# Opening of a fused attention and mixture-of-experts kernel: first tokens loaded first and in halves, two of four norms on VectorE, two Toeplitz matrices loaded directly, the transposes of the queries ahead of the first unit

## The reference

```python
q  = layernorm(x)                       # over the 256 positions
kv = einsum('bhil,bhjl->bijhl', ctx, ctx)        # 16 heads of 8 channels
y  = causal_convolution(kv, ssm_kernel) + kv * D # along l, one filter and one D per head
x  = x + tanh(g_xattn) * einsum('bijhl,bihl->bjhl', y, q)
x  = x + tanh(g_ffn) * (experts(layernorm(x)) + shared_expert(layernorm(x)))
```

## Time and profile before

| what | value |
|---|---|
| median of 3 runs | 236.66 us (236.22 to 240.86) |
| profiled execution | 237.96 us, its span 236.1 us |
| PE busy | 199.6 us (85%) |
| DVE busy | 146.7 us (62%) |
| POOL busy | 121.3 us (51%) |
| ACT busy | 81.8 us (35%) |
| DMA | 31.87 MB, 135 GB/s over the span |

### The profile page before, as it was taken

One profiled execution on the slowest core, in us unless ns is written; L12 is line 12 of the kernel. 1 busy time (PEld: TensorE's weight loads), 2 busy tenths in 40 slices (PEclk: granted clock), 3 DMA queues, 4 the chain that ended last, 5 costly groups with the idle time before them and its releaser, 6 DMA issues.

```text
span 236.1 us, 3938 instructions
## 1 busy us (share of the span) xinstructions
PE 199.6 (85%) x1344; PEld 180.4 (76%) x1344; DVE 146.7 (62%) x479; ACT 81.8 (35%) x155; POOL 121.3 (51%) x125
## 2 busy tenths in 40 slices
PE   0195699977999799999999899897879989999940
PEld 0173579966999699898998898795779989899830
DVE  2508689589788987579855844652455665556220
ACT  2071440517434471333333165131443234423100
POOL 1497755267754789415850270260353757545642
PEclk9999799999999999999999999999999999999995
DMA  6599972000000020020501994897524798431311
GB/s 209 144 326 370 390 269 89 0 0 0 4 3 3 0 90 3 0 90 3 178 0 64 326 270 170 264 306 220 159 66 107 230 292 241 165 109 59 94 38 44
DMA packets 23925, 31.87 MB, mean 135 GB/s; under 512 B 3214, under 2 KB 21398, under 8 KB 23904
## 3 DMA queue, kind: packets, MB, share of 16 engines
q1 hardware_dynamic: 21312, 24.77, 33.2%
q0 software_dynamic: 2304, 6.05, 7.6%
q10 hardware_dynamic: 288, 0.79, 1.0%
HBM read 21.32 MB, written 10.54 MB: 135 GB/s over the span
## 4 chain that ended last, share of the span: by engine, by line
PE 63%; DMA 13%; issue 7%; DVE 7%; ACT 3%; SPq 2%; POOL 2%; POOLq 1%; DVEq 0%; ACTq 0%
PE fb L1084 12%; PE z L1000 10%; PE tp L1023 9%; PE z L1084 8%; PE z L1098 7%; PE fb L1098 7%; PE z L997 6%; DMA x_sb<-x 4%; DMA kv<-xd_scratch 4%; DMA xd_scratch<-xrow,dest 2%; DVE terms L428 2%; PE tp L1109 1%; DMA kskip_scratch<-kp 1%; ACT wh_gu L730 1%; DVE stats L782 1%
## 5 line engine op out<-in xcount | busy, mean ns | idle before, releaser
L428 DVE TENSOR_TENSOR terms<-z,qr 128x512 f32<-128x512 f32 (+2 forms) x192 | 48.8, 327 | 15.3 <-PE z L1000 8.5
L997 PE MATMUL z<-kv,toep 128*128 128x144 f32 x128 | 28.4, 305 | 19.4 <-DMA toep<-kskip_scratch 11.1
L997 PEld LDWEIGHTS z<-kv,toep 128*128 128x128 f32 x128 | 23.3, 200 | 26.9 <-issue 20.5
L1000 PE MATMUL z<-kv,toep 128*128 128x288 f32 x128 | 43.6, 424 | 0.0
L409 POOL TENSOR_TENSOR kv<-ct 128x768 f32<-128x768 f32 x15 | 28.1, 1871 | 16.4 <-PE z L1000 14.9
L1084 PE MATMUL fb<-xTh,wh_gu 128*128 128x256 f32 (+1 forms) x104 | 32.4, 311 | 1.8 <-issue 1.8
L1084 PE MATMUL fb<-xTl,wh_gu 128*128 128x256 f32 (+1 forms) x104 | 29.0, 279 | 0.0
L1084 PE MATMUL fb<-xTh,wl_gu 128*128 128x256 f32 (+1 forms) x104 | 29.0, 279 | 0.0
L619 POOL DMA_INDIRECT kv<-base_scratch,tok x16 | 19.8, 1235 | 16.0 <-DMA base_scratch<-x_sb 10.6
L630 POOL DMA_INDIRECT out<-kv,tok x16 | 16.1, 1004 | 21.9 <-DVE kv L887 18.7
L1084 PE MATMUL z<-xTh,wh_gu 128*128 128x256 f32 (+1 forms) x88 | 26.0, 295 | 1.2 <-DVE xTl L904 1.2
(11 more groups left out here) (108 smaller groups left out, 382.8 us busy)
## 6 DMA issues: line engine op xcount, KB each, us to landing
terms<-w SPq DMA_DIRECT2D x16, 352.0 KB, 4.6
...
```

The source lines that it names most:

```text
L428: return eng.tensor_tensor(view(terms, t0 + row * TROW + col, [[64, 2], *td]), view(src, zo, [[512, 2], *zd]), view(qr, q0 + qo, [[CW, 2], ...
L997: pe.matmul(view(z[s % 2], k * 512 + GB, [[PL, NPL], [1, GB]]), toep[:, h, P:2 * P], view(kv, o, [[PL, NPL], [1, GB]]), start=True, stop=F ...
L1000: mm = pe.matmul(z[s % 2][:, k, 0:KVH], toep[:, h, 0:P], view(kv, o, [[1, KVH]]), start=False, stop=True, skip_group_check=True)
```

## The change

Seven edits, all of them ahead of slot 4:

1. x of group 0 is SP's first transfer and comes as two transfers of two sequences (`x_half`, `x_in[0]`). DVE takes the statistics of the first two when the first is there. Filters and D are issued by ACT, ahead of the context.
2. The Toeplitz matrices of heads 0 and 1 are loaded straight from the filters as they come in, and D is put on their diagonals in SBUF: DVE adds `anti` (a matrix with ones where the diagonal lies, made by POOL) times D to the left half of each. The load through HBM covers heads 2 and 3, then four heads each as before.
3. x of group 1 is issued before the store of the corrected filters. The context of group 1 is issued ahead of the matrices of heads 8 to 15, and the three small loads behind them.
4. ACT norms two of the first four sequences, DVE the other two (`tensor_scalar`, a new line), after DVE's planes.
5. POOL makes `anti`, and computes one power of ones ahead of the first real one.
6. PE turns the queries of group 0 ahead of the convolution of slot 0.
7. ACT's tanh of the gates stands in slot 4 in place of ahead of slot 0.

The store of the filters has 768 KB more ahead of it on this queue than before, and the context and x of group 1 have moved up. The diff, without the declarations and the renumbered waits on POOL's constants:

```diff
@@ -383,6 +390,8 @@
 
             what, g = norms[n]
             eng.wait_ge(xn_done if what == "ln1" else xrow_done, g + 1)
+            if n == 0:
+                eng.wait_ge(xn_dve, 1)
 
         def load_rows(sp, e):
             if e == 0:
@@ -453,13 +462,18 @@
                 sp.dma_start(ct[:, g % 2, :], ctxt[g]).then_inc(ctx_in[g], 16)
 
             def load_x(g):
+                if g == 0:
+                    for i, done in ((0, x_half), (2, x_in[0])):
+                        sp.dma_start(x_sb[:, i:i + 2, :], x[i:i + 2].rearrange("b c l -> c b l")).then_inc(done, 16)
+                    return
                 sp.dma_start(x_sb[:, GB * g:GB * (g + 1), :],
                              x[GB * g:GB * (g + 1)].rearrange("b c l -> c b l")).then_inc(x_in[g], 16)
 
             def load_toeplitz(k):
 
-                src = bass.AP(kskip.tensor, kskip.offset + 4 * k * KPAD, [[1, P], [KPAD, 4], [1, L]])
-                sp.dma_start(toep[:, 4 * k:4 * k + 4, :], src).then_inc(toep_in[k], 16)
+                h, n = (4 * k, 4) if k else (2, 2)
+                src = bass.AP(kskip.tensor, kskip.offset + h * KPAD, [[1, P], [KPAD, n], [1, L]])
+                sp.dma_start(toep[:, h:h + n, :], src).then_inc(toep_in[k], 16)
 
             def load_gu(dst, a1, a3, done):
                 for m, a in ((0, a1), (1, a3)):
@@ -487,20 +501,22 @@
                 load_gu(gu_set[e % SETS], w1[e], w3[e], gu_in[e % SETS])
                 load_tail(down_set[e % SETS], w2[e], down_in[e % SETS], 0)
 
-            sp.dma_start(kp[:, :], kpad).then_inc(skip_in, 16)
-            sp.dma_start(dcol[:, :], bass.AP(skip_d.tensor, skip_d.offset, [[1, H], [1, 1]])).then_inc(skip_in, 16)
             load_x(0)
+            sp.dma_start(d_bc[:, :], bass.AP(skip_d.tensor, skip_d.offset, [[0, P], [1, 2]])).then_inc(d_in, 16)
+            sp.dma_start(toep[:, 0:2, :],
+                         bass.AP(kpad.tensor, kpad.offset, [[1, P], [KPAD, 2], [1, L]])).then_inc(toep_first, 16)
+            load_x(1)
             sp.wait_ge(skip_added, 1)
             sp.dma_start(kskip, kp[:, :]).then_inc(skip_stored, 16)
             sp.wait_ge(skip_stored, 16)
             load_toeplitz(0)
+            load_toeplitz(1)
+            load_ctx(1)
+            load_toeplitz(2)
+            load_toeplitz(3)
             sp.dma_start(gates[:, 0:1], bass.AP(g_x.tensor, g_x.offset, [[0, P], [1, 1]])).then_inc(small_in, 16)
             sp.dma_start(gates[:, 1:2], bass.AP(g_f.tensor, g_f.offset, [[0, P], [1, 1]])).then_inc(small_in, 16)
             sp.dma_start(wg_sb[:, :, :], wg.rearrange("(k p) e -> p k e", p=P)).then_inc(small_in, 16)
-            for k in range(1, 4):
-                load_toeplitz(k)
-            load_ctx(1)
-            load_x(1)
             load_shared_gu()
             load_tail(shared_down, sw2, shared_down_in, AGAIN)
             load_x(2)
@@ -552,6 +568,11 @@
             chain(pool.memset(ident[:, :], 0.0))
             pool.affine_select(out=ident[:, :], in_=ident[:, :], compare_op=ALU.not_equal, fill=1.0, base=0,
                                pattern=[[-1, P]], channel_multiplier=1).then_inc(pool_consts, 1)
+            chain(pool.memset(anti[:, :], 0.0))
+            pool.affine_select(out=anti[:, :], in_=anti[:, :], compare_op=ALU.not_equal, fill=1.0, base=1 - P,
+                               pattern=[[1, P]], channel_multiplier=1).then_inc(pool_consts, 1)
+            chain(pool.memset(rstd[:, :], 1.0))
+            chain(pool.tensor_tensor(rstd[:, :], rstd[:, :], rstd[:, :], ALU.pow))
             pool.wait_ge(dve_consts, 5)
             scale_and_bias(0)
             kv_place_free(pool, 0, 1)
@@ -638,7 +659,7 @@
                 what, g = norms[n]
                 act.wait_ge(rstd_done, n + 1)
                 free()
-                for b in range(GB):
+                for b in range(2 if n == 0 else GB):
                     last = act.activation(dst(b), x_sb[:, GB * g + b, :], ACT.Identity,
                                           bias=nbias[:, b:b + 1], scale=rstd[:, b:b + 1])
                 last.then_inc(xn_done if what == "ln1" else xrow_done, 1)
@@ -729,15 +750,18 @@
                     act.wait_ge(f_ready, gu_last(8 + e - 2) + 1)
                 act.activation(wh_gu[w % 2][:, 0:GUW], gu_set[e % SETS], ACT.Copy).then_inc(w_high, 1)
 
+            act.dma_start(kp[:, :], kpad).then_inc(skip_in, 16)
+            act.dma_start(dcol[:, :], bass.AP(skip_d.tensor, skip_d.offset, [[1, H], [1, 1]])).then_inc(skip_in, 16)
             act.dma_start(ct[:, 0, 0:4 * CW], ctxt[0, :, 0:4 * CW]).then_inc(ctx_first, 16)
             act.dma_start(ct[:, 0, 4 * CW:], ctxt[0, :, 4 * CW:]).then_inc(ctx_in[0], 16)
             norm1(0)
             for c in range(1, 4):
                 squares(0, c)
             q_copy(0)
-            act.wait_ge(small_in, 16 * 3)
-            act.activation(tg[:, :], gates[:, :], ACT.Tanh).then_inc(tanh_done, 1)
             for s in range(SLOTS):
+                if s == ROUTER_SLOT:
+                    act.wait_ge(small_in, 16 * 3)
+                    act.activation(tg[:, :], gates[:, :], ACT.Tanh).then_inc(tanh_done, 1)
                 if s in SHARED_AT:
                     silu(FU_AT[SHARED_AT[s]])
                 if kv_due(s)[0] >= 0:
@@ -779,6 +803,8 @@
                 if n >= 1:
                     dve.wait_ge(rstd_done, n)
                 for b in range(GB):
+                    if n == 0 and b % 2 == 0:
+                        dve.wait_ge(x_in[0] if b else x_half, 16)
                     ins = dve.bn_stats(stats[:, b, :], x_sb[:, GB * g + b, :])
                 chain(ins)
                 for b in range(GB):
@@ -932,10 +958,19 @@
 
             dve.wait_ge(skip_in, 32)
             dve.tensor_tensor(kp[:, P - 1:P], kp[:, P - 1:P], dcol[:, :], ALU.add).then_inc(skip_added, 1)
-            dve.wait_ge(x_in[0], 16)
             norm_stats(0)
             dve.wait_ge(ctx_first, 16)
             kv_products(dve, 0, 0, 0, kv_dve)
+            dve.wait_ge(rstd_done, 1)
+            for b in range(2, GB):
+                ins = dve.tensor_scalar(xn[:, b, :], x_sb[:, b, :], rstd[:, b:b + 1], nbias[:, b:b + 1], ALU.mult, ALU.add)
+            ins.then_inc(xn_dve, 1)
+            dve.wait_ge(pool_consts, 2)
+            dve.wait_ge(d_in, 16)
+            dve.wait_ge(toep_first, 16)
+            for h in range(2):
+                dve.scalar_tensor_tensor(out=toep[:, h, 0:P], in0=anti[:, :], scalar=d_bc[:, h:h + 1],
+                                         in1=toep[:, h, 0:P], op0=ALU.mult, op1=ALU.add).then_inc(diag_added, 1)
             for s in range(SLOTS):
                 for k in range(2):
                     if due(f"residual{k}", s) >= 0:
@@ -986,7 +1021,9 @@
                 else:
                     pe.wait_ge(kv_pool, 4 * g + i)
                     pe.wait_ge(kv_square, 4 * g + i)
-                if g == 0 and u % 2 == 0:
+                if s == 0:
+                    pe.wait_ge(diag_added, 2)
+                elif g == 0 and (s == 1 or u % 2 == 0):
                     pe.wait_ge(toep_in[u // 2], 16)
                 if s >= 2:
                     pe.wait_ge(prods, s - 1)
@@ -1003,6 +1040,8 @@
 
             def turn_q(g):
                 pe.wait_ge(xn_done, g + 1)
+                if g == 0:
+                    pe.wait_ge(xn_dve, 1)
                 for k in range(BLK):
                     n = TP_AT[("q", g, k)]
                     tp_wait(pe, n)
@@ -1111,8 +1150,8 @@
                 mm.then_inc(tp_ready, 1)
 
             pe.wait_ge(pool_consts, 1)
+            turn_q(0)
             convolve(0)
-            turn_q(0)
             for s in range(SLOTS):
                 if 1 <= s < CONV:
                     convolve(s)
```

13 lines of the change are left out of this document (10 added, 3 removed).

## The result

Over 20 runs each on the same chip the changed kernel took 235.07 us in the median (233.35 to 238.82) and the kernel before 238.02 (235.39 to 240.86): a ratio of 0.9895, 95% interval 0.9867 to 0.9923. The ratios here leave out runs that lie over 1.5% above the fastest of their kernel, so they are not the quotients of the medians. Timed again later, 12 runs beside 23, the ratio was 0.9918 (0.9881 to 0.9954). So the change makes the kernel faster by about 1%, 2 to 3 us, where 4.1 was forecast. The profiled execution spans 234.2 us (before 236.1).

The account below looks back on a forecast made before the run. It took a late start of PE's and DVE's lists as the bound; successive shifts at slots 0, 2 and 4 left slot 6 4.1 us earlier, turning the 236.66 median into 232.5 us, range 230.2 to 235.3.

Parts of the forecast that it names:

- x of group 0, the power, the norms: Start of group 0: POOL starts the power at 7.15, ACT can begin at about 8.45 instead of 11.46, 3.0 us earlier.
- The block: DVE's norms of group 0 wait for POOL's planes, ending at 11.0 instead of 9.5; slot 0 gains only 1.0 us.
- x of group 1: Ahead of slot 2: DVE's 1.11 us wait for this load goes, statistics start at 19.3, slot 2 starts 2.4 us earlier.
- The clock: PE's pause before slot 4 shrinks to 2.4 us, keeping full clock; slot 4 takes 1.46 not 2.94, starting 4.1 us earlier.
- The context of group 1: Lands at 17.2 where POOL waited until 20.00, leaving POOL just off the path; slot 6 at 28.8, 4.1 us earlier.
- The third rival: Matrices' trip through HBM is late, context of group 1 lands at 20: gain 2.5 us, 234.2; chance 0.10.
- The second and third rivals: Clock falls again at slot 4 (gain 2.6, 234.1, chance 0.11) and late matrices' trip through HBM (0.10); both together 235.5.
- No block: First rival: DVE's norms end at 9.5 without waiting for POOL, slot 0 at 14.0; gain 5.0 to 5.4, 231.4; chance 0.28.
- Slower: Slot 1 waits for matrices of heads 2 and 3, landing as late as 19.2: 237.5, or 238.5; chance 0.03.
- Lost later: The shift is lost in the transfers from 30 us on, leaving a gain between nothing and 4 us; chance 0.04.
- one of the prediction's own signs: PE waiting for `toep` in slots 1 to 6 would show the forecast wrong.

Follow-up runs that it names:

- a filler: The kernel before with eight extra 128x256 matmuls of constants on PE between the convolutions of slots 3 and 4: ratio 0.9997.
- the kernel without the two slow transfers: Changed kernel, D of heads 0 and 1 set to 1 instead of loaded, direct Toeplitz load replaced by 256 KB of x: one run, 233.33 us.
- the hole filled: Changed kernel with the context of group 1 issued right behind the filters' store, ahead of the wait for its landing: ratio 0.9870, median 234.57 us.
- all of it together: Changed kernel, filters' store before x, x and context of group 1 before its wait, 26 matmuls before first transposes, four before slot 4: 0.9840, 233.78 us.

## Why the prediction was right or wrong

**x of group 0, the power, the norms: right.** Statistics ended at 6.84 (7.0 forecast), set by the first addition (4.69, behind the filters and D), not by x. The power started at 7.02 (7.15) and took 1.01. One thing was missed: POOL's bias, 0.2 us by itself, took 1.12 because DVE was on its planes. The lock works in that direction too, and ACT began at 9.26, not 8.45.

**The block: right in kind, other in place.** The norms didn't wait (0.73 for both; 0.3 each was taken), since the context reached POOL only at 9.82. The diagonals waited instead. The transposes began at 10.46 (11.0), slot 0 at 15.71 (16.2). The gain at slot 0 is 1.5 us, of which I had 1.0.

**x of group 1: right.** No wait, statistics from 19.35 (19.3), slot 2 at 21.66 (21.6).

**The clock: the step that failed.** "I take it that 2.4 does not" made one level of the clock before and the other after, from two pauses of a single execution, and put 1.5 us of the 4.1 on it. What it said of the changed kernel held in three of four profiles: slot 4 at 23.86 to 24.68, where 24.7 was forecast. What failed was the other side of the difference. The kernel before kept its clock too in one of its two profiles, with slot 4 at 26.92 and not 28.86, and a filler that kept it there gained at most about 1 us in the timed runs (0.9997). Over the 64 timed runs of the kernel before that the comparisons use the mean granted clock was 0.9823, over 31 of the changed one 0.9843. If a run is at either full or half clock, that is 8.3 and 7.3 us at half; one microsecond less there is worth 0.5 us, not the 1.5 of the sum. The means of these runs are 237.45 and 235.26. Of the 2.2 us between them 0.5 is the clock by that estimate, and the 0.9 to 1.7 us of the full-clock profiles is the earlier start. That the two add up is arithmetic on different executions, not an experiment.

Part of these 8.3 and 7.3 us lies in the last slice, which is low in every page, and part near 164 us, so the mean doesn't say how often slot 4 is hit.

**The context of group 1: late, the second step that failed.** It was taken at 19.42 against 17.2 forecast. The store landed 6.6 us after its issue at 4.87, at 11.5 and not at 9.5, behind transfers at a third of the rate I gave them. The two slow transfers explain 0.6 to 1.2 us of these 2; without them the store still took 5.6 us. And all that SP issues behind it waits for its return. With the clock full this is what binds: PE waits 1.16 us for the norm of group 1, and slot 6 gains 1.4 us less than slot 4; with the context issued ahead of that wait the 1.4 us were back. The third rival named this mechanism with 0.10.

**What came to the same.** The second and third rivals together were put at 235.5; the median was 235.07. That match is half luck: the forecast stood on a median of 236.66 from three runs, and 20 runs, those three among them, gave 238.02. Against one and the same kernel before, the gain was 2.95 us (2.2 between the means above) where 4.1 was forecast, and slot 6 in the profile is 2.34 earlier, what one of the two rivals gives. **No block** was not what happened, but the kernel without the two slow transfers shows it: slot 0 at 13.68 against 14.0 worked out. **Slower** did not occur: slot 1's matrices were in time in every profile of the changed kernel to within 0.5 us. They were not at 13, though: they landed at about 15.4 in two of the profiles, and PE waited 0.26 to 0.48 us for `toep` in slot 1 or 2 in three of the four, one of the prediction's own signs.

**Lost later: no** up to 118 us. Behind that the traces differ from one execution to the next: from the issue of the last scatter of tokens, at about 152 us, to that of the last store it takes 75.1 us before, 75.4 after, 74.2 with the hole filled and 77.5 with all of it together, although nothing there was edited. The fall of the clock near 164 us is a part of it: the changed kernel takes 75.0 and 75.4 without it and 75.8 and 76.3 with it, and all of it together, with 77.5, has the longest. So that run's profiled time of 236.23 us, over its median of 233.78, says little of its edits.

Open: what decides whether the clock falls at a given pause, and how the 2.2 to 2.95 us of the timed runs divide, since the fair profiles give 0.9 to 1.7 us at slot 6. The filler ahead of slot 4 kept the clock there in all five profiles that had it, and the timed runs show no gain from it beyond their intervals. The context of group 1 ahead of the wait together with all four norms on ACT wasn't tried.
